# Transposing ternary FFN weights by DMA instead of on TensorE, with the layer-norm transposes in f32

## The chip, the cores and the metric

The kernel runs on the 8 cores of one Trainium2 chip. Each core computes two of the 16 sequences of the batch and exchanges nothing with the others; every core prepares the weights for itself. The metric is the device time in microseconds of the slowest core.

## The reference

A transformer block without an output projection, over x of shape (16, 4096, 1024):

```python
xn = _layernorm(x, axis=-1)
x = x + attn(xn, Wq, bq, Wk, bk, Wv, bv) + ffn(xn, W1, b1, W2, b2)
...
def _ternary(w):
    scale = jnp.maximum(jnp.mean(jnp.abs(w)), 1e-08)
    return jnp.clip(jnp.round(w / scale), -1.0, 1.0)      # value in the forward pass
h = gelu(x @ _ternary(W1).T + b1)        # W1: (4096, 1024)
out = h @ _ternary(W2).T + b2            # W2: (1024, 4096)
```

The attention is full width (one head of 1024), with the scores masked to zero above the diagonal before the softmax. The kernel computes the row sums of the softmax and scales each token's own V row with their ratio to themselves; that part is the same in both versions.

## The kernel before, in words

A core owns 8192 tokens, in 32 supertiles of 256 (`NSUP`), handled in 16 pairs. The code writes one list of operations for each engine with a small emitter: `E(...)` adds a compute operation, `DMA(...)` a transfer. Each names what it reads and writes, and the emitter works out the semaphore waits. The order in a list is the order of emission, and all instructions are issued at one line (L708 in the profile), so groups are told apart by tile names. A `DMA` also waits until the semaphore it is given has seen its previous transfer finish (L96 and L97). SP issues the loads of weights, x and cached keys; POOL (GpSimd) issues the stores and the second weight stream of the preparation.

The order of the program (L673 to L692): x of supertiles 0 and 1 and their layer-norm statistics, attention of pair 0, the preparation of the weights (`emit_prep`), and then for every pair u: FFN of supertile 2u-2, FFN of 2u-1, attention of pair u; at last the FFNs of the last pair.

`emit_prep` (L228) has three passes over tiles of 1 MB of f32 weights, 16 tiles each. Pass one loads W1 (SP) and sums the absolute values on ScalarE, which gives the threshold. Pass two loads W1 again, makes each tile ternary with two VectorE operations (`tern_tile`, L256), transposes it in 16 blocks of 128x128 on TensorE into PSUM, and ScalarE copies it into `w1t_sb`, where all of W1 transposed stays for the rest of the kernel. Beside it POOL loads W2 into one of two halves of `ktbuf` and ScalarE sums it. Pass three (L315) loads W2 again, makes it ternary, transposes it on TensorE, ScalarE copies it into `ktbuf`, and POOL stores it transposed to HBM, in `w2t` of shape (4096, 1024).

`emit_ffn` (L568) handles one supertile. For each of 32 slices f of the hidden layer: `emit_h(f)`, 8 matmuls of 256 columns with `w1t_sb` and a GELU on ScalarE into `hT`; `emit_o2(f)`, 4 matmuls of 512 columns of `hT` with `w2buf` into `ps_o2a` and `ps_o2b`. `w2buf` holds two chunks of W2 transposed, each good for two slices; chunk k+2 is loaded from `w2t` (`load_w2chunk`, L575) once `emit_o2(2k+1)` has freed its place:

```python
emit_o2(f - 2)
if (f - 2) % 2 == 1 and (f - 2) // 2 + 2 < 16:
    load_w2chunk((f - 2) // 2 + 2)
if f == 4:
    emit_v(1)
emit_h(f)
```

`emit_v` (L625) is the V projection of 128 tokens with the fused residual.

`emit_ln_finish` (L392) normalizes x into `xnbf` in bf16 and keeps a bf16 copy of x in `xbfres`. `emit_attn_pair` (L429) transposes `xnbf` on TensorE into PSUM, viewed as bf16, and VectorE copies it into `xnt`; then come Q, K and the scores. For the second half of a pair, `emit_ln_finish` stands inside `emit_attn_pair`.

Of the kernel before, what the change touches and what calls it, by code (L numbers as in the profile page):

```python
# [14 lines left out]
D = 1024  # L15
FF = 4096
# [85 lines left out]
def build_program(nc, B, SEQ):  # L102
# [15 lines left out]
    id_h = nc.dram_tensor("ident", [128, 128], BF16, kind="ExternalInput")  # L118
# [6 lines left out]
    w2t_h = nc.dram_tensor("w2t", [FF, D], BF16, kind="Internal")  # L125
# [19 lines left out]
    xnbf = sb("xnbf", [128, 2048], BF16)  # L145
# [15 lines left out]
    ident = sb("ident_sb", [128, 128], BF16)  # L161
# [12 lines left out]
    psqk_bf = ps_qk[:].bitcast(BF16)  # L174
    pss_bf = ps_s[:].bitcast(BF16)
# [52 lines left out]
    def emit_prep():  # L228
# [24 lines left out]
        t1v, t1k = w2buf[:, 0:2048], ["w2buf:0"]  # L253
# [14 lines left out]
        for tt in range(16):  # L268
# [6 lines left out]
            tbf = psqk_bf if tt % 2 == 0 else pss_bf  # L275
            tkeys = ["psqk:0", "psqk:1"] if tt % 2 == 0 else ["pss:0", "pss:1"]
            grp = []
            for u in range(2):
                for j in range(NJ):
                    k = u * NJ + j  # L280
                    grp.append(("transpose",
                                (tbf[:, k * 128:(k + 1) * 128],
                                 wtv[:, u * 1024 + j * 128:u * 1024 + (j + 1) * 128],
                                 ident[:]), {}))
            E("tensor", None, None, group=grp, reads=wtk + ["ident"], writes=tkeys)
            for u in range(2):
                E("scalar", "copy",
                  (w1t_sb[:].rearrange("p (j f) -> p j f", j=NJ)[:, :, (tt * 2 + u) * 128:(tt * 2 + u + 1) * 128],
                   tbf[:, u * 1024:(u + 1) * 1024].rearrange("p (j c) -> p j c", j=NJ)),
                  reads=tkeys, writes=["w1t"])  # L290
            ktf32 = ktbuf[:].bitcast(F32)
            j2, qq2p = divmod(tt, 2)
            buf2 = ktf32[:, (tt % 2) * 2048:(tt % 2 + 1) * 2048]
            bkey2 = [f"ktbuf:{tt % 2}"]
            DMA("gpsimd", s_gp[tt % 4], buf2,
# [4 lines left out]
              reads=bkey2, writes=["dump:0", "dump:1", f"acc:{tt}"])  # L300

# [13 lines left out]
        for qq2 in range(2):  # L315
            for j in range(NJ):
                tt = qq2 * 8 + j
                buf, bkey = pB(tt % 2), pkeys[tt % 2][0:2]
                DMA("sync", s_pl[tt % 4], buf,
                    w2_h.ap()[j * 128:(j + 1) * 128, qq2 * 2048:(qq2 + 1) * 2048],  # L320
                    writes=bkey)
                wtv, wtk = tern_tile(buf, bkey[0], 2, 3, tt % 2)
                tbf = psqk_bf if tt % 2 == 0 else pss_bf
                tkeys = ["psqk:0", "psqk:1"] if tt % 2 == 0 else ["pss:0", "pss:1"]
                grp = []
                for fs in range(16):
                    grp.append(("transpose",
                                (tbf[:, fs * 128:(fs + 1) * 128],
                                 wtv[:, fs * 128:(fs + 1) * 128],
                                 ident[:]), {}))  # L330
                E("tensor", None, None, group=grp, reads=wtk + ["ident"], writes=tkeys)
                stage = ktbuf[:, (j % 2) * 4096:(j % 2) * 4096 + 2048]
                skey = f"ktbuf:{j % 2}"
                E("scalar", "copy", (stage, tbf[:, 0:2048]),
                  reads=tkeys, writes=[skey])
                DMA("gpsimd", s_gp[tt % 4],
# [342 lines left out]
    if NSUP > 2:  # L679
        emit_x_loads(2)  # L680
    emit_prep()
    for u in range(1, NP):
# [5 lines left out]
        if 2 * u + 2 < NSUP:  # L688
            emit_x_loads(2 * u + 2)
# [68 lines left out]
```

How the kernel before makes its waits and increments, by code:

```python
        def go(eng):  # L702
            for waits, group, (s, amt) in lst:
                for ws, wv in waits:
                    eng.wait_ge(ws.h, wv)
                last = None
                for method, args, kwargs in group:
                    last = getattr(eng, method)(*args, **kwargs)
                if last is not None and s is not None:
                    last.then_inc(s.h, amt)
```

## Time and profile before

| | us |
|---|---|
| time, median of 2 runs | 3693.57 (3692.96 to 3694.18) |
| time of the profiled execution | 3707.41 |
| span of its slowest core (core 7) | 3705.9 |
| spans of its eight cores | 3645.7 to 3705.9 |
| TensorE busy in it | 3179.7 (86%) |
| ScalarE, VectorE busy in it | 1153.2, 559.8 |

The profile is of one execution and one core, the slowest; times in it count from the start of the span. PE is TensorE, PEld its weight loads, DVE VectorE, ACT ScalarE, SPq the queue of DMA issues on SP. The granted clock is a share of the full one.

### The profile page before, as it was taken

The page shows a single profiled execution, that of the slowest core. Times are in us where ns is not written, and L with a number is a line of the kernel's source. Part 1 is how long each engine was busy: PE and PEld are TensorE (multiplying, and loading weights), DVE is VectorE, ACT ScalarE, POOL GpSimd, SP SyncE. Part 2 cuts the span into 40 slices and gives each one's busy share as a digit, 9 for nine tenths or more (in the row PEclk, how much of TensorE's full clock was granted, in tenths as well). Part 3 has the DMA queues.
Part 4 walks back from the last instruction along what each step waited for, and adds up shares of the span by engine and source line. Part 5 has one row for each costly group of instructions (what it writes and reads, how often), then busy time and mean ns, then how long its engine had stood idle before and what let it go on. Part 6 is the DMA issues. An engine that isn't in the chain of part 4 may idle for free.

```text
span 3705.9 us, 57742 instructions; the slowest of 8 cores (3645.7 to 3705.9 us)
## 1 busy us (share of the span) xinstructions
PE 3179.7 (86%) x21512; PEld 2054.4 (55%) x21512; DVE 559.8 (15%) x1036; ACT 1153.2 (31%) x2414; POOL 97.9 (3%) x135
## 2 busy tenths in 40 slices
PE   3123899999998989999899989899898999989899
PEld 2122566665665565556555656566565565555655
DVE  1055211102011100201002020201110110101000
ACT  1453323232333232332323223233323233332332
POOL 0001000000000000000000000000000000000000
PEclk9555899999999999999999999999999999999999
DMA  6798533425252443424434252525243333534334
GB/s 126 215 293 252 170 126 117 145 92 160 78 158 85 148 120 112 156 74 156 121 105 160 86 166 75 171 75 165 75 152 121 120 120 108 162 95 137 114 110 141
DMA packets 298512, 496.66 MB, mean 134 GB/s; under 512 B 14596, under 2 KB 129284, under 8 KB 294150
## 3 DMA queue, kind: packets, MB, share of 16 engines
q1 hardware_dynamic: 276694, 411.19, 35.8%
q0 software_dynamic: 21552, 81.80, 7.3%
q8 instruction: 183, 3.00, 0.3%
q14 instruction: 83, 0.68, 0.1%
HBM read 440.50 MB, written 58.72 MB: 135 GB/s over the span
## 4 chain that ended last, share of the span: by engine, by line
PE 71%; DMA 19%; DVE 4%; issue 3%; ACT 2%; SPq 0%; DVEq 0%; ACTq 0%; POOL 0%; POOLq 0%
PE ps_qk L708 37%; PE ps_s L708 12%; PE ps_o2a L708 11%; PE ps_o2b L708 10%; DMA w2buf<-w2t 9%; DMA ktbuf<-kthbm 4%; ACT dump L708 2%; DMA xld<-w 2%; DMA outst<-w 2%; DMA xld<-x 1%; DVE w2buf L708 1%; DVE xnbf L708 1%; DVE xnt L708 1%; DVE outst L708 1%; DVE dump L708 1%
## 5 line engine op out<-in xcount | busy, mean ns | idle before, releaser
L708 PE MATMUL ps_qk<-xnt,w1t_sb 128*128 128x256 bf16 x8192 | 1060.8, 273 | 18.4 <-DVE msk L708 18.4
L708 PEld LDWEIGHTS ps_qk<-xnt,w1t_sb 128*128 128x128 bf16 x8192 | 800.9, 98 | 325.4 <-issue 24.0
L708 ACT ACTIVATE hT<-ps_qk,b1l 128x256 bf16<-128x256 f32 x1024 | 482.2, 474 | 1529.7 <-PE ps_qk L708 1529.3
L708 PE MATMUL ps_o2a<-w2buf,hT 128*128 128x512 bf16 x2048 | 610.0, 379 | 52.3 <-DMA w2buf<-w2t 50.7
L708 PE MATMUL ps_o2b<-w2buf,hT 128*128 128x512 bf16 x2048 | 609.8, 379 | 0.0
L708 PEld LDWEIGHTS ps_o2b<-w2buf,hT 128*128 128x128 bf16 x2048 | 200.1, 98 | 242.6 <-issue 1.1
L708 PE MATMUL ps_qk<-xnt,wq_sb 128*128 128x256 bf16 x2048 | 257.6, 294 | 18.5 <-DVE xnt L708 18.5
L708 PEld LDWEIGHTS ps_o2a<-w2buf,hT 128*128 128x128 bf16 x2048 | 189.0, 98 | 121.3 <-issue 99.7
L708 PE MATMUL ps_s<-ktbuf,qt 128*128 128x512 bf16 x896 | 214.8, 395 | 44.2 <-DMA ktbuf<-kthbm 44.0
L708 DVE TENSOR_SCALAR sts<-sts 128x1 f32<-128x1 f32 (+1 forms) x194 | 29.3, 152 | 1466.4 <-ACT dump L708 1457.6
L708 PEld LDWEIGHTS ps_qk<-xnt,wq_sb 128*128 128x128 bf16 x2048 | 214.7, 105 | 61.1 <-issue 22.3
L708 PE MATMUL ps_s<-wv_sb,xnt 128*128 128x512 bf16 x1024 | 243.2, 380 | 0.0
L708 PE MATMUL ps_qk<-xnt,wk_sb 128*128 128x256 bf16 x2048 | 226.2, 273 | 0.0
L708 PEld LDWEIGHTS ps_qk<-xnt,wk_sb 128*128 128x128 bf16 x2048 | 200.4, 98 | 23.2
L708 PE MATMUL ps_qk<-ktbuf,qt 128*128 128x512 bf16 x896 | 202.5, 379 | 0.0
L708 PEld LDWEIGHTS ps_s<-ktbuf,qt 128*128 128x128 bf16 x896 | 89.0, 101 | 161.6 <-issue 71.2
L708 ACT ACTIVATE qt<-ps_qk,bql 128x512 bf16<-128x512 f32 x128 | 88.0, 688 | 286.1 <-PE ps_qk L708 286.1
L708 PE MATMUL ps_qk<-ident_sb,xnbf 128*128 128x128 bf16 x512 | 50.3, 265 | 146.7 <-DVE xnbf L708 146.6
L708 DVE TENSOR_TENSOR msk<-ps_s,trilm_sb 128x128 bf16<-128x128 f32 x32 | 9.3, 292 | 1013.7 <-PE ps_s L708 1003.3
L708 PEld LDWEIGHTS ps_s<-wv_sb,xnt 128*128 128x128 bf16 x1024 | 89.6, 98 | 119.7 <-issue 29.0
L708 PEld LDWEIGHTS ps_qk<-ktbuf,qt 128*128 128x128 bf16 x896 | 87.6, 98 | 105.7
L708 ACT ACTIVATE ktcur<-ps_qk,bkl 128x512 bf16<-128x512 f32 x128 | 88.0, 687 | 135.6 <-PE ps_qk L708 135.6
(70 smaller groups left out, 1615.5 us busy)
## 6 DMA issues: line engine op xcount, KB each, us to landing
w2buf<-w2t SPq DMA_DIRECT2D x512, 512.0 KB, 3.7
ktbuf<-kthbm SPq DMA_DIRECT2D x112, 512.0 KB, 4.7
xld<-x SPq DMA_DIRECT2D x64, 512.0 KB, 5.5
out<-outst POOLq DMA_DIRECT2D x64, 512.0 KB, 3.7
outst<-w SPq DMA_DIRECT2D x24, 1024.0 KB, 7.5
xld<-w SPq DMA_DIRECT2D x24, 1024.0 KB, 7.4
kthbm<-ktcur POOLq DMA_DIRECT2D x32, 512.0 KB, 3.9
ktbuf<-w POOLq DMA_DIRECT2D x16, 1024.0 KB, 8.2
```

Source lines behind the costliest of these rows:

```text
L708: last = getattr(eng, method)(*args, **kwargs)
```

## The change

It does four things. The ternary W1 is no longer transposed on TensorE: POOL stores each ternary tile as it is to `w1tern`, and when all 16 are stored, SP issues eight DMA transposes of 4096x128 each into `w1t_sb`. The ternary W2 is stored as it is to `w2tern`, and each chunk that an FFN loads is now two DMA transposes of 1024x128, issued by SP on the one semaphore of that chunk's place. In pass two the W2 stream has one buffer (`xld`) and not two halves of `ktbuf`. The layer norm writes f32 in place over x in `xld`, after the copy to `xbfres`; the transposes of it are f32, go to `ps_qk` and `ps_s` in turn, and `ident` is f32. Because `xld` now holds the normalized x until it is transposed, the loads of x for the next pair stand behind the attention.

```diff
@@ emit_prep, pass two
-            E("tensor", None, None, group=grp, reads=wtk + ["ident"], writes=tkeys)
-            for u in range(2):
-                E("scalar", "copy",
-                  (w1t_sb[...], tbf[:, u * 1024:(u + 1) * 1024]...),
-                  reads=tkeys, writes=["w1t"])
+            DMA("gpsimd", s_gp[tt % 4],
+                w1tern_h.ap()[tt * 256:(tt + 1) * 256, :].rearrange("(two p) c -> p two c", p=128),
+                wtv.rearrange("p (two c) -> p two c", two=2),
+                reads=wtk, writes=[f"w1tern:{tt}"])
-            buf2 = ktf32[:, (tt % 2) * 2048:(tt % 2 + 1) * 2048]
-            bkey2 = [f"ktbuf:{tt % 2}"]
+            buf2 = xld[:, 0:2048]
+            bkey2 = ["xld00", "xld01"]
...
+        for j in range(NJ):
+            DMA("sync", s_tp[j % 2], w1t_sb[:, j * FF:(j + 1) * FF],
+                w1tern_h.ap()[:, j * 128:(j + 1) * 128],
+                reads=[f"w1tern:{t}" for t in range(16)], writes=["w1t"], transpose=True)
@@ emit_prep, pass three
-                E("tensor", None, None, group=grp, reads=wtk + ["ident"], writes=tkeys)
-                E("scalar", "copy", (stage, tbf[:, 0:2048]), reads=tkeys, writes=[skey])
-                DMA("gpsimd", s_gp[tt % 4], w2t_h.ap()[...], stage..., reads=[skey], writes=[f"w2t:{qq2}:{j}"])
+            DMA("gpsimd", s_gp[tt % 4],
+                w2tern_h.ap()[j2 * 128:(j2 + 1) * 128, qq2p * 2048:(qq2p + 1) * 2048],
+                wtv,
+                reads=wtk, writes=[f"w2tern:{qq2p}:{j2}"])
@@ emit_ln_finish
-            E("vector", "tensor_scalar",
-              (xnbf[:, i * 1024:(i + 1) * 1024], buf, mean, rstd, ALU.subtract, ALU.mult),
-              reads=[bkey, meank, rstdk], writes=[f"xnbf:{i}"])
             E("vector", "tensor_copy",
               (xbfres[:, p * 2048 + i * 1024:p * 2048 + (i + 1) * 1024], buf),
               reads=[bkey], writes=[f"xbfres:{p}:{i}"])
+            E("vector", "tensor_scalar",
+              (buf, buf, mean, rstd, ALU.subtract, ALU.mult),
+              reads=[bkey, meank, rstdk], writes=[bkey])
@@ emit_attn_pair
-                                (psqk_bf[:, i * 1024 + j * 128:i * 1024 + (j + 1) * 128],
-                                 xnbf[:, i * 1024 + j * 128:i * 1024 + (j + 1) * 128],
+                                (pst[:, j * 128:(j + 1) * 128],
+                                 xbuf[:, j * 128:(j + 1) * 128],
                                  ident[:]), {}))
@@ load_w2chunk
-            DMA("sync", s_w2[wb],
-                w2buf[:, wb * 2048:(wb + 1) * 2048].rearrange("p (ft c) -> p ft c", ft=2),
-                w2t_h.ap()[k * 256:(k + 1) * 256, :].rearrange("(ft p) c -> p ft c", p=128),
-                reads=[f"w2t:{k // 8}:{j}" for j in range(NJ)], writes=[f"w2buf:{wb}"])
+            for u in range(2):
+                ft = 2 * k + u
+                DMA("sync", s_w2[wb],
+                    w2buf[:, wb * 2048 + u * 1024:wb * 2048 + (u + 1) * 1024],
+                    w2tern_h.ap()[:, ft * 128:(ft + 1) * 128],
+                    reads=[f"w2tern:{ft // 16}:{j}" for j in range(NJ)],
+                    writes=[f"w2buf:{wb}"], transpose=True)
@@ order of the program
+        emit_attn_pair(u)
         if 2 * u + 2 < NSUP:
             emit_x_loads(2 * u + 2)
-        emit_attn_pair(u)
```

The queue of SP, with its waits, at the start of the first FFN before the change; `s_w20` and `s_w21` are the semaphores of the two places in `w2buf`, sP is TensorE's, sV VectorE's, `s_gp0` to `s_gp3` those of POOL's transfers:

```order
63 L708 DMA w2buf<-w2t 128x2x1024 [waits s_gp0,s_gp1,s_gp2,s_gp3,sV,sP]
64 L708 DMA w2buf<-w2t 128x2x1024 [waits sV]
65 L708 DMA w2buf<-w2t 128x2x1024 [waits s_w20,sP]
66 L708 DMA w2buf<-w2t 128x2x1024 [waits s_w21,sP]
67 L708 DMA w2buf<-w2t 128x2x1024 [waits s_w20,sP]
```

The same place in SP's queue after the change:

```order
71 L687 DMA_TRANSPOSE w2buf<-w2tern 128x1024 [waits s_gp0,s_gp2,sV]
72 L687 DMA_TRANSPOSE w2buf<-w2tern 128x1024 [waits s_w20]
73 L687 DMA_TRANSPOSE w2buf<-w2tern 128x1024 [waits sV]
74 L687 DMA_TRANSPOSE w2buf<-w2tern 128x1024 [waits s_w21]
75 L687 DMA_TRANSPOSE w2buf<-w2tern 128x1024 [waits s_w20,sP]
76 L687 DMA_TRANSPOSE w2buf<-w2tern 128x1024 [waits s_w20]
77 L687 DMA_TRANSPOSE w2buf<-w2tern 128x1024 [waits s_w21,sP]
```

Each load has become two, and the second of a chunk stands behind a wait for the first one's semaphore.

VectorE's queue in the first attention pair before the change, from the first half's layer norm to the last copy of a transpose:

```order
L708 TENSOR_SCALAR xnbf<-xld,sts 128x1024
L708 CAST xbfres<-xld 128x1024
L708 TENSOR_SCALAR xnbf<-xld,sts 128x1024
L708 CAST xbfres<-xld 128x1024
L708 COPY xnt<-ps_qk 128x8x128 x2
```

And VectorE's queue for the same half after the change:

```order
L687 CAST xbfres<-xld 128x1024
L687 TENSOR_SCALAR xld<-xld,sts 128x1024
L687 CAST xbfres<-xld 128x1024
L687 TENSOR_SCALAR xld<-xld,sts 128x1024
L687 CAST xnt<-ps_qk 128x8x128
L687 CAST xnt<-ps_s 128x8x128
```

The copy to `xbfres` now stands ahead of the operation that the transposes wait for, and the copies from PSUM read f32.

## Rows read from the trace of the kernel before

**Rows 1.** The page: busy tenths and granted clock in 40 slices.

```profile
PE 3179.7 (86%) x21512; PEld 2054.4 (55%) x21512; DVE 559.8 (15%) x1036; ACT 1153.2 (31%) x2414; POOL 97.9 (3%) x135
...
PEclk9555899999999999999999999999999999999999
```

**Rows 2.** Waits by engine, in us, times and longest: TensorE on `w2buf`.

```profile
PE ps_o2a L708 <- DMA w2buf<-w2t: 50.7, 66, 2.4
```

**Rows 3.** Timeline of TensorE, 701 to 709 us: start, duration, group, idle before.

```profile
701.81 0.59 PE L708 MATMUL ps_o2a<-w2buf,hT 128*128 128x512 bf16 x2
...
704.54 0.59 PE L708 MATMUL ps_o2a<-w2buf,hT 128*128 128x512 bf16 x2 [0.83 <-DMA w2buf<-w2t]
704.97 0.59 PE L708 MATMUL ps_o2b<-w2buf,hT 128*128 128x512 bf16 x2
705.40 1.04 PE L708 MATMUL ps_qk<-xnt,w1t_sb 128*128 128x256 bf16 x8
706.27 0.59 PE L708 MATMUL ps_o2a<-w2buf,hT 128*128 128x512 bf16 x2
```

**Rows 4.** DMA issues of the whole run: count, KB each, median us to landing.

```profile
w2buf<-w2t SPq DMA_DIRECT2D x512, 512.0 KB, 3.7
...
ktbuf<-w POOLq DMA_DIRECT2D x16, 1024.0 KB, 8.2
w2t<-ktbuf POOLq DMA_DIRECT2D x16, 512.0 KB, 6.6
```

**Rows 5.** The tile `w2buf`: its loads' shortest, median and longest time to landing.

```profile
DMA to landing us min/median/max: 3.3/3.7/9.0
```

**Rows 6.** Stretches holding two FFNs: busy us, granted clock, DMA share, GB/s.

```profile
390.00:455.00 65.00, 63.56 (x407) 38.55 (x405) 5.03 (x6) 15.93 (x34) 0.88 (x1) 1.00 0.46 138
455.00:520.00 65.00, 63.45 (x412) 39.39 (x411) 10.78 (x18) 18.94 (x41) 1.43 (x2) 1.00 0.49 152
```

**Rows 7.** Stretches holding passes two and three of the preparation, same columns.

```profile
182.00:296.00 114.00, 30.57 (x260) 26.64 (x260) 58.65 (x35) 62.40 (x64) 7.40 (x14) 0.50 0.89 285
296.00:387.00 91.00, 29.79 (x257) 26.24 (x258) 59.02 (x33) 27.99 (x15) 17.12 (x15) 0.50 0.83 249
```

**Rows 8.** Groups by form: busy us, mean ns of one, idle before.

```profile
L708 DVE SCALAR_TENSOR_TENSOR dump<-xld,sts,w2buf 128x2048 bf16<-128x2048 f32 x16 | 37.6, 2351 | 11.0 <-ACT dump L708 9.2 <-DVE w2buf L708 1.7
L708 ACT ACTIVATE dump<-ktbuf 128x2048 bf16<-128x2048 f32 x16 | 30.6, 1912 | 0.0
L708 PE MATMUL ps_s<-sts,onesf 1*128 1x2 f32 x4 | 1.1, 345 | 1.5 <-DVE sts L708 1.5
L708 DVE SCALAR_TENSOR_TENSOR outst<-ps_o2a,outst 128x1024 f32<-128x1024 f32 x32 | 39.2, 1224 | 97.2 <-PE ps_o2b L708 97.2
```

**Rows 9.** Timeline of one pair's transposes on TensorE and VectorE, 709 to 720 us.

```profile
709.80 1.06 PE L708 MATMUL ps_qk<-ident_sb,xnbf 128*128 128x128 bf16 x16
713.84 1.47 DVE L708 COPY xnt<-ps_qk 128x1024 bf16<-128x1024 bf16 x2
715.23 0.80 DVE L708 TENSOR_SCALAR xnbf<-xld,sts 128x1024 bf16<-128x1024 f32 x1
715.95 0.68 DVE L708 CAST xbfres<-xld 128x1024 bf16<-128x1024 f32 x1
716.28 1.01 PE L708 MATMUL ps_qk<-ident_sb,xnbf 128*128 128x128 bf16 x8 [5.42 <-DVE xnbf L708]
...
719.74 2.51 PE L708 MATMUL ps_qk<-xnt,wq_sb 128*128 128x256 bf16 x11 [1.12 <-DVE xnt L708]
```

**Rows 10.** Stretches around that pause: busy us by engine, granted clock, DMA share.

```profile
708.00:712.00 4.00, 2.86 (x26) 1.59 (x23) 1.18 (x7) 2.96 (x6) 0.00 (x0) 1.00 0.66 214
...
716.00:720.00 4.00, 2.29 (x18) 1.78 (x19) 3.25 (x6) 0.00 (x0) 0.00 (x0) 0.50 0.99 351
720.00:724.00 4.00, 4.00 (x21) 2.83 (x20) 0.00 (x0) 0.59 (x1) 0.00 (x0) 0.50 0.85 231
724.00:728.00 4.00, 4.00 (x35) 3.46 (x34) 0.00 (x0) 1.11 (x3) 0.00 (x0) 0.92 0.56 215
```

More of the change, by code:

```diff
@@ L124, in build_program @@
     w2tern_h = nc.dram_tensor("w2tern", [D, FF], BF16, kind="Internal")
-    w2t_h = nc.dram_tensor("w2t", [FF, D], BF16, kind="Internal")
     ctx = ExitStack()
@@ L274, in emit_prep @@
             wtv, wtk = tern_tile(buf, bkey[0], 0, 1, tt % 2)
-            tbf = psqk_bf if tt % 2 == 0 else pss_bf
-            tkeys = ["psqk:0", "psqk:1"] if tt % 2 == 0 else ["pss:0", "pss:1"]
-            grp = []
-            for u in range(2):
[L279 to L284, printed above, removed]
-            E("tensor", None, None, group=grp, reads=wtk + ["ident"], writes=tkeys)
-            for u in range(2):
-                E("scalar", "copy",
-                  (w1t_sb[:].rearrange("p (j f) -> p j f", j=NJ)[:, :, (tt * 2 + u) * 128:(tt * 2 + u + 1) * 128],
-                   tbf[:, u * 1024:(u + 1) * 1024].rearrange("p (j c) -> p j c", j=NJ)),
-                  reads=tkeys, writes=["w1t"])
-            ktf32 = ktbuf[:].bitcast(F32)
+            DMA("gpsimd", s_gp[tt % 4],
+                w1tern_h.ap()[tt * 256:(tt + 1) * 256, :].rearrange("(two p) c -> p two c", p=128),
+                wtv.rearrange("p (two c) -> p two c", two=2),
+                reads=wtk, writes=[f"w1tern:{tt}"])
             j2, qq2p = divmod(tt, 2)
-            buf2 = ktf32[:, (tt % 2) * 2048:(tt % 2 + 1) * 2048]
-            bkey2 = [f"ktbuf:{tt % 2}"]
-            DMA("gpsimd", s_gp[tt % 4], buf2,
+            buf2 = xld[:, 0:2048]
+            bkey2 = ["xld00", "xld01"]
+            DMA("gpsimd", s_gp[(tt + 2) % 4], buf2,
                 w2_h.ap()[j2 * 128:(j2 + 1) * 128, qq2p * 2048:(qq2p + 1) * 2048],
@@ L314, in emit_prep @@
         E("vector", "tensor_copy", (thrbc[:, 2:4], ps_s[:, 10:12]), reads=["pss:0"], writes=["thrbc"])
[L315 to L330, printed above, removed]
-                E("tensor", None, None, group=grp, reads=wtk + ["ident"], writes=tkeys)
[L332 to L336, printed above, removed]
-                    w2t_h.ap()[qq2 * 2048:(qq2 + 1) * 2048, j * 128:(j + 1) * 128].rearrange(
-                        "(fs p) c -> p fs c", p=128),
-                    stage.rearrange("p (fs c) -> p fs c", fs=16),
-                    reads=[skey], writes=[f"w2t:{qq2}:{j}"])
+        for tt in range(16):
+            j2, qq2p = divmod(tt, 2)
+            buf, bkey = pB(tt % 2), pkeys[tt % 2][0:2]
+            DMA("sync", s_pl[tt % 4], buf,
+                w2_h.ap()[j2 * 128:(j2 + 1) * 128, qq2p * 2048:(qq2p + 1) * 2048],
+                writes=bkey)
+            wtv, wtk = tern_tile(buf, bkey[0], 2, 3, tt % 2)
+            DMA("gpsimd", s_gp[tt % 4],
+                w2tern_h.ap()[j2 * 128:(j2 + 1) * 128, qq2p * 2048:(qq2p + 1) * 2048],
+                wtv,
+                reads=wtk, writes=[f"w2tern:{qq2p}:{j2}"])
     NSUP = B * NST
@@ L441, in emit_attn_pair @@
             for i in range(2):
+                pst = ps_qk if i == 0 else ps_s
+                tkeys = ["psqk:0", "psqk:1"] if i == 0 else ["pss:0", "pss:1"]
+                xbuf = xld[:, p * 2048 + i * 1024:p * 2048 + (i + 1) * 1024]
                 grp = []
@@ L678, in build_program @@
     emit_attn_pair(0)
+    emit_prep()
     if NSUP > 2:
         emit_x_loads(2)
-    emit_prep()
     for u in range(1, NP):
```

16 lines of the change are left out of this document (6 added, 10 removed).

## The prediction

> **What bounds the kernel now.** I read the slices first. TensorE is busy eight or nine tenths of every slice but the first four, and there its granted clock falls to half (1.2 instead of 2.4 GHz) [rows 1]. So the kernel has two parts: a preparation of weights in which transfers and VectorE set the pace, and some 3300 us in which TensorE sets it. The waits come second. TensorE waits for `w2buf` only 50.7 us in all, 66 times, 2.4 us at most [rows 2]. The loads of W2 are therefore hidden, but barely. The timeline shows how barely. One chunk of `w2buf` serves two slices, and a slice takes 0.87 us for `emit_o2` and 0.87 us for `emit_h`: 704.54 to 705.40 and 705.40 to 706.27 [rows 3]. A slice is 704.54 to 706.27, 1.73 us, and a chunk lasts 3.47 us. From the moment its place is free until the chunk is needed again TensorE has three `emit_h` and two `emit_o2` to do, 5 x 0.87 = 4.34 us, and the load lands in 3.7 us [rows 4]. The margin is 0.6 us, and where a load is late, TensorE stands, 0.83 us in one place [rows 3]. An FFN takes about 65 us [rows 6], 32 of them 2080 us. Anything that lengthens a chunk's load past 4.3 us is paid on the path, up to 512 times.
>
> **W2 by DMA transposes.** A chunk is now two transposes, and the second is not issued before the first has landed, because both use the semaphore of their place. Call T the time from issue to landing of one transpose of 256 KB. A place goes through T + T for the load and then `emit_o2`, `emit_h`, `emit_o2`, 2.6 us, until it is free. Two places alternate, so a chunk can't come more often than every P = (2T + 2.6)/2 = T + 1.3 us. SP waits with everything behind it while a first half is in flight, which sets P no shorter than T and adds nothing. P stays within 3.47 us only if T is 2.2 us, and a late chunk is avoided altogether only if T is 2.17 us, half of 4.34.
>
> The trace has no DMA transpose, so T must be bounded. From below: the plain load of 512 KB lands in 3.7 us [rows 4], and 256 KB at the same rate would be 1.85 us. From above: the longest landing of any load into `w2buf`, 9.0 us [rows 5], for a transfer that shares its engines badly. The nearest row is the store `w2t<-ktbuf`, 512 KB cut into pieces of 256 bytes: 6.6 us [rows 4]. The transpose reads pieces of 256 bytes as well (128 columns of bf16), half as many: between 3.3 us if the time goes by pieces and 6.6 us if it doesn't. I take the middle, T = 5.0 us.
>
> What TensorE does then matters too. With T = 5.0 and full clock P is 6.3 us and TensorE stands 2.8 us of it in one piece. In this trace a pause of 0.83 us costs no clock, while one of 5.42 us does: the granted clock is 0.50 from 716 to 724 us and back at 0.92 only in the next stretch, after 4 us and more of dense work [rows 9, 10]. In the preparation, where TensorE is busy 27% of the time in short pieces, it is 0.50 throughout [rows 7]. An FFN of 3.5 us of work and 2.8 us of pause lies between these rows, nearer to the preparation in its pattern. I take half clock. Then the work between landing and free place is 5.2 us and P = T + 2.6 = 7.6 us.
>
> An FFN pair has 32 chunks, of which the first two of the FFN that follows an attention are loaded under that attention. So a pair costs 30 x P + 6 us (the two `emit_h` and the V projection ahead of the first chunk). For 16 pairs: 16 x (30 x 7.6 + 6) = 3744 us, against 2080 us now. Term: +1664 us. With full clock it is 16 x (30 x 6.3 + 6) = 3120, +1040 us.
>
> At this place the Trainium skill speaks against itself. "Advanced Engine Details and Errata", section X-Bar Transpose (TRN2), has transposes as fast as ordinary transfers, at 350 to 400 GB/s; by it 256 KB are 0.75 us on the wire, and T would be that of a plain load (rival two). "VectorE: DVE Perf Modes", section The three transpose paths, gives 1309 ns for one 128x128 block by DMA; eight of them in a row would be 10.5 us, and the estimate of the whole would lie above rival three. No run here shows either yet.
>
> **The preparation.** Pass two takes 114 us and its transfers run at 285 GB/s [rows 7]. It loses the TensorE transposes and 32 ScalarE copies, which lie beside the transfers and give nothing back while these set the pace. It gains 8 MB of stores. The W2 stream has one buffer now, so load, sum and next load are a chain: for two tiles two loads of 8.2 us [rows 4], two sums of 1.9 + 0.2 us, a ternary operation of 2.35 us [rows 8] between them (the odd tile goes to `dump`, which the sum also writes, and POOL issues in order), and about 2 us of issues: 25 us, 200 us for the pass, +86 us. If loads land faster with fewer in flight, nothing is lost. I take +55 us, between 0 and 86.
>
> The eight transposes of W1 are 8 MB, 32 times 256 KB, two in flight: 32 x 5.0 / 2 = 80 us. SP does nothing else meanwhile and pass three's loads are queued behind it, so all of it is on the path; bounds 30 us (T = 1.85) and 144 us (T = 9.0). Pass three takes 91 us [rows 7], set by load and VectorE (59 of its 91 us busy); TensorE and ScalarE leave it and that gives nothing. Its first two loads are no longer under way when the threshold is known, and the first FFN must wait for a store and two transposes: +10 us, between 0 and 20. Together +145 us.
>
> **The layer norm.** Moving x's loads behind the attention costs nothing: they are needed at the end of the next FFN, 65 us later. On the path is the stretch from the end of an FFN to the Q projection, 709.80 to 719.74 us, 16 times (in the first pair TensorE has no FFN before it) [rows 9]. Three things grow. The copy to `xbfres` now precedes the normalization (+0.68 us). The copies out of PSUM read f32: 1.22 us, as the row that reads 1024 f32 from PSUM has it [rows 8], for 0.69 us. And the transposes are f32: eight in bf16 take 1.01 us [rows 9]; the two f32 matmuls of the preparation stand in the trace as four [rows 8], so a factor of two is the least likely to be missed; I bound the group by 1.01 and 4 us and take 3 us. Followed through: first half done at 715.8, second copy until 717.0, CAST and normalization until 718.5, two groups of 3 us until 724.5, copy until 725.7. That is +6 us for a pair, +96 us for 16 (bounds 0.7 and 10 us, 11 and 160 us).
>
> **Sum.** 3707.4 + 1664 + 145 + 96 = 5612 us for the profiled execution. The median of the runs is 13.8 us below the profiled one, so 5598; I say 5600 us.
>
> **The rivals.**
> One, T near the low end by pieces, 3.3 us, with full clock because the pauses are 1.1 us. P = 4.6, the FFNs take 16 x (30 x 4.6 + 6) = 2304, +224; preparation 55 + 53 + 10; layer norm 96. Total +438: 4130 us. For it: the DMA engines are busy only 0.46 of an FFN [rows 6]. Between it and the forecast lies T = 5.0 with full clock, 3694 + 1040 + 145 + 96 = 4975 us.
> Two, the other side: transposes land like plain transfers, T under 2.2 us, and stay hidden in the 4.34 us between a free place and its use. Then the FFNs keep their 2080 us, W1 costs 30, the layer norm 11: 3735 us, within 2% of now; if the 50.7 us of waits went as well, 3684. It decides at T = 2.17 us. Against it: no load of 512 KB landed in under 3.3 us [rows 5], and two latencies in a row have to fit.
> Three, a transpose is worked off slowly, T = 9.0 us or more. P = 11.6 at half clock, the FFNs take 16 x (30 x 11.6 + 6) = 5664, +3584; preparation 55 + 144 + 10; layer norm 96: 7580 us. For it: small pieces on both sides, 1024 rows read and columns of two bytes written, on eight cores at once.
>
> **How the numbers follow.** The forecast and its surroundings, 4700 to 6700 us (T from 4 to 7, either clock), 0.45. Rival one, 3900 to 4700, 0.22. Rival three, above 6700, 0.30. Rival two 0.03. The range goes from 4150 us (a little above rival one) to 7700 us (a little above rival three at 9.0 us), which leaves out about 2 in 10. A measurement of this kernel can tell some 2% from no change. Slower by more than that 0.96, within 0.03, faster 0.01.
>
> **What would show it.** In the changed kernel: `w2buf<-w2tern` with 1024 issues and its time to landing, which is T itself; TensorE's waits for `w2buf` in the thousands of us instead of 50.7; the granted clock in an FFN, 0.5 for my forecast and 1.0 for rival one; SPq waiting for `w2buf` transfers and not for TensorE. Chunk to chunk the timeline should show T + 1.3 or T + 2.6 us. The layer norm's stretch should be about 16 us long instead of 10, and a stretch of some 80 us with only DMA work should stand between passes two and three. The prediction is wrong if T is below 2.2 us, or if several transposes in flight slow each other so that P follows the rate and not T; then T itself grows in the trace.

## The result and the profile after

The changed kernel takes 4839.34 us (median of 11 runs, 4827.84 to 5025.98) against 3693.5 us (10 runs) for the kernel before on the same chips: a ratio of 1.3112 (95% interval 1.3084 to 1.314), 1146 us more. The profiled execution took 4831.11 us, with a span of 4829.6 us on its slowest core (core 3). In some runs the cores of one die (four of the eight) showed a much lower clock than the other four; comparisons leave these runs out, and where an experiment's profile was such a run I read a core of the other die.

The page of the changed kernel, its parts 1, 2 and 4:

```profile
PE 3383.1 (70%) x21000; PEld 2088.6 (43%) x21000; DVE 603.4 (12%) x1036; ACT 1092.0 (23%) x2366; POOL 100.2 (2%) x151
...
PE   3000377787777878777787877787777878778787
...
PEclk9555689899999999899899999999999989999999
...
DMA packets 1275924, 513.57 MB, mean 106 GB/s; under 512 B 1120900, under 2 KB 1235716, under 8 KB 1271558
...
DMA w2buf<-w2tern 36%; PE ps_qk L687 21%; PE ps_s L687 8%; PE ps_o2a L687 6%; PE ps_o2b L687 5%; DMA xld<-w 3%; DMA ktbuf<-kthbm 3%; SPq L687 3%; ACT dump L687 2%; DVE xnt L687 1%; DMA w1t_sb<-w1tern 1%; DMA outst<-w 1%; DVE w2buf L687 1%; DVE outst L687 0%; DMA w2tern<-w2buf 0%
```

TensorE's tenths fall from eight and nine to seven and eight [rows 1], and the busiest piece of the chain that ends last is now the transposed loads of W2, 36% of the span. The clock row matters as much: it doesn't stay at half speed in the FFNs, as I had forecast, but near nine tenths. The waits say who stands. "SPq" is SP's issuing of DMAs; its two rows are its waits ahead of an issue:

```profile
PE ps_o2a L687 <- DMA w2buf<-w2tern: 853.5, 366, 100.5
...
PE ps_qk L687 <- DVE xld L687: 150.4, 17, 65.2
...
SPq L684 <- DMA w2buf<-w2tern: 1392.6, 512, 8.3
SPq L684 <- PE ps_o2b L687: 710.3, 200, 49.7
```

TensorE waits 853.5 us for `w2buf`, 50.7 before [rows 2]. The longest, 100.5 us, isn't in an FFN: it is the first `emit_o2` standing until the preparation is over. About 753 us are left, 702 more than before [rows 2]. SP waits for `w2buf` transfers 512 times, exactly once per chunk: that is the second half held back until the first has landed, 2.7 us at a time.

The groups of the FFN's matmuls (busy us, mean ns of one, idle before):

```profile
L687 PE MATMUL ps_qk<-xnt,w1t_sb 128*128 128x256 bf16 x8192 | 1149.4, 288 | 71.5 <-DMA w1t_sb<-w1tern 53.0
L687 PE MATMUL ps_o2a<-w2buf,hT 128*128 128x512 bf16 x2048 | 667.6, 410 | 709.3 <-DMA w2buf<-w2tern 709.1
...
L687 PE MATMUL ps_o2b<-w2buf,hT 128*128 128x512 bf16 x2048 | 669.0, 411 | 0.0
```

The same instructions took 1060.8, 610.0 and 609.8 us before. So they cost 205 us more of busy time, which is the clock at half speed in part of the FFN. Waits (702) and clock (205) make 907 us. The timeline gives the growth itself: the 16 pairs of FFNs, each from its first `emit_h` to its last `emit_o2` (the first pair from its first `emit_o2`, so without that long wait), take 3096 us in all against 2157 before, 939 more; the stretches between them (the attention) take 28 us more, and the first `emit_o2` starts 157 us later. Together that is the 1124 us between the two spans.

How long a transpose takes stands in two views, part 6 of the page and the tile `w2buf` (duration in ns of the issue on SP, then us to landing):

```profile
w2buf<-w2tern SPq DMA_TRANSPOSE x1024, 3.6
...
w1t_sb<-w1tern SPq DMA_TRANSPOSE x8, 7.7
```

```profile
L687 SPq DMA_TRANSPOSE w2buf<-w2tern x1024: 1143/1147/2776, 542.5 to 4815.6; - x171
...
DMA to landing us min/median/max: 3.0/3.6/12.0
```

T, the time from issue to landing of one transpose, has a median of 3.6 us. The chain of waits at one place in the first FFN pair shows how two of them stack up (start, us, what):

```profile
604.34 4.83 DMA w2buf<-w2tern
609.24 4.21 DMA w2buf<-w2tern
613.45 0.14 issue
613.58 1.01 PE ps_o2a L687 x2
614.59 0.85 PE ps_o2b L687 x2
615.45 1.69 PE ps_qk L687 x8
617.13 0.43 PE ps_o2a L687 x2
617.56 0.45 PE ps_o2b L687 x2
618.04 0.04 issue
618.08 5.00 DMA w2buf<-w2tern
```

Two landings in a row, 9.0 us; then `emit_o2`, `emit_h`, `emit_o2`, 4.5 us; then the place is free and the next first half is issued. That is 13.74 us for two chunks, P = 6.87, where P is the time from chunk to chunk. It is one of the slow ones. Over chunks 4 to 15 of all 32 FFNs a chunk comes every 5.6 us: the two landings take 3.76 and 3.55 us in the mean, the work from `emit_o2` to the free place 3.0 us, and about 0.9 us lies between them (between the halves, from landing to `emit_o2`, from the free place to the next issue). 314 of these 384 chunks are late by more than 0.2 us. The first `emit_o2` and the `emit_h` after it run at half clock (1.01 us and 1.69 us), the second one at full clock again. The timeline of TensorE later in the run shows that this is not always so:

```profile
2791.99 1.01 PE L687 MATMUL ps_o2a<-w2buf,hT 128*128 128x512 bf16 x2 [3.68 <-DMA w2buf<-w2tern]
...
2795.03 0.59 PE L687 MATMUL ps_o2a<-w2buf,hT 128*128 128x512 bf16 x2
...
2804.17 0.59 PE L687 MATMUL ps_o2a<-w2buf,hT 128*128 128x512 bf16 x2 [3.76 <-DMA w2buf<-w2tern]
...
2806.83 1.06 PE L687 MATMUL ps_o2a<-w2buf,hT 128*128 128x512 bf16 x2
2807.68 0.92 PE L687 MATMUL ps_o2b<-w2buf,hT 128*128 128x512 bf16 x2
```

After these pauses of 3.7 us the clock is at half speed for some 3 us, at once or a little later, and full again. Behind a pause of 2.50 us a little earlier (2779.44 us) the same two matmuls take 0.59 us, so it stays full there. The stretches of the preparation (pass two, the W1 transposes, pass three):

```profile
182.00:377.00 195.00, 0.00 (x0) 0.00 (x0) 55.13 (x31) 30.03 (x30) 21.86 (x31) 0.50 0.58 196
380.00:440.00 60.00, 0.74 (x4) 0.61 (x4) 0.62 (x4) 2.00 (x2) 0.00 (x0) 0.50 0.84 151
440.00:542.00 102.00, 8.27 (x34) 3.80 (x34) 58.12 (x32) 2.13 (x3) 9.38 (x15) 0.53 0.84 255
```

Pass two takes 195 us (114 before), the transposes 60, pass three 102 (91 before) [rows 7]. In pass two the DMA engines are now busy 0.58 instead of 0.89: a chain has replaced a rate. The first `emit_o2` starts at 552.4 instead of 395.6 us, 157 us later. Last, the layer norm between FFN and attention:

```profile
763.70 1.04 PE L687 MATMUL ps_qk<-ident_sb,xld 128*128 128x128 f32 x8
...
766.25 1.22 DVE L687 CAST xnt<-ps_qk 128x1024 bf16<-128x1024 f32 x1
...
770.64 1.94 PE L687 MATMUL ps_qk<-ident_sb,xld 128*128 128x128 f32 x8 [5.03 <-DVE xld L687]
...
775.86 1.36 PE L687 MATMUL ps_qk<-xnt,wq_sb 128*128 128x256 bf16 x11 [1.65 <-DVE xnt L687]
```

From the first transpose to the Q projection it takes 12.2 us, 9.9 before [rows 9]. The f32 transposes take twice the time of the bf16 ones. At full clock eight of them take 1.04 us, where before the change sixteen took 1.06 us (709.80 us in [rows 9]); at half clock eight take 1.94 us, where before they took 1.01 us (716.28 us there, with a granted clock of 0.50 in [rows 10]). From start to start it is 109 against 56 ns at full clock, and 217 against 100 ns at half.

### The profile page after: what moved, and what is told of

The parts are those of the page before. It is cut to its first block, busy times and chain, and to the rows that moved or that the text cites. A ratio compares the mean times of both kernels' runs of the same rounds, so it can differ in the third digit from the quotient of the medians.

```text
span 4829.6 us, 57552 instructions; the slowest of 8 cores (4705.6 to 4829.6 us)
## 1 busy us (share of the span) xinstructions
PE 3383.1 (70%) x21000; PEld 2088.6 (43%) x21000; DVE 603.4 (12%) x1036; ACT 1092.0 (23%) x2366; POOL 100.2 (2%) x151
## 4 chain that ended last, share of the span: by engine, by line
DMA 47%; PE 41%; DVE 4%; SPq 3%; issue 3%; ACT 2%; DVEq 0%; ACTq 0%; POOL 0%; POOLq 0%
DMA w2buf<-w2tern 36%; PE ps_qk L687 21%; PE ps_s L687 8%; PE ps_o2a L687 6%; PE ps_o2b L687 5%; DMA xld<-w 3%; DMA ktbuf<-kthbm 3%; SPq L687 3%; ACT dump L687 2%; DVE xnt L687 1%; DMA w1t_sb<-w1tern 1%; DMA outst<-w 1%; DVE w2buf L687 1%; DVE outst L687 0%; DMA w2tern<-w2buf 0%
## 5 line engine op out<-in xcount | busy, mean ns | idle before, releaser
L687 PE MATMUL ps_qk<-xnt,w1t_sb 128*128 128x256 bf16 x8192 | 1149.4, 288 | 71.5 <-DMA w1t_sb<-w1tern 53.0
L687 PE MATMUL ps_o2a<-w2buf,hT 128*128 128x512 bf16 x2048 | 667.6, 410 | 709.3 <-DMA w2buf<-w2tern 709.1
L687 PEld LDWEIGHTS ps_qk<-xnt,w1t_sb 128*128 128x128 bf16 x8192 | 846.3, 104 | 451.5 <-issue 146.4
L687 PE MATMUL ps_o2b<-w2buf,hT 128*128 128x512 bf16 x2048 | 669.0, 411 | 0.0
L687 PEld LDWEIGHTS ps_o2b<-w2buf,hT 128*128 128x128 bf16 x2048 | 213.0, 104 | 284.4 <-issue 74.3
L687 PE MATMUL ps_qk<-xnt,wq_sb 128*128 128x256 bf16 x2048 | 241.9, 283 | 26.8 <-DVE xnt L687 26.8
L687 ACT ACTIVATE dump<-xld 128x1024 bf16<-128x1024 f32 (+1 forms) x88 | 112.5, 1281 | 204.1 <-DMA xld<-w 193.5
L687 PE MATMUL ps_qk<-ident_sb,xld 128*128 128x128 f32 x256 | 48.5, 353 | 150.4 <-DVE xld L687 150.4
```

Source lines behind the costliest of these rows:

```text
L687: last = getattr(eng, method)(*args, **kwargs)
```

## The experiments

Twelve kernels ran. Times are of the whole kernel, and each ratio is to the kernel before, run beside it (3684 to 3691 us). A difference between two kernels is the difference of their ratios times 3690 us.

### The two halves of a chunk

**e1_own_sem.** The changed kernel, with a semaphore and a key of its own for each half of a place. `emit_o2(f)` waits for its own half and frees it by itself.

```diff
-    s_w2 = [em.sem("s_w20"), em.sem("s_w21")]
+    s_w2 = [em.sem(f"s_w2{i}") for i in range(4)]
...
-                DMA("sync", s_w2[wb],
+                DMA("sync", s_w2[2 * wb + u],
...
-                    writes=[f"w2buf:{wb}"], transpose=True)
+                    writes=[f"w2buf:{wb}:{u}"], transpose=True)
...
-            reads = [f"hT:{bank}", f"w2buf:{wb}"]
+            reads = [f"hT:{bank}", f"w2buf:{wb}:{f % 2}"]
```

> The changed kernel, with a semaphore and a tile key for each half of a chunk, so that SP issues the second transpose of a chunk right behind the first and does not wait for its landing. Theory chain (the loss in the FFNs is two landings in a row, 4.85 and 4.12 us in the chain of waits of the changed kernel): a chunk then lands 1.15 us (the issue) + 4.5 us = 5.7 us after its place is free, not 9.0, and chunks can come every (5.7 + 2.6) / 2 = 4.2 us. Most of the 930 us goes: 3900 to 4100 us in all. Theory rate (the crossbar or the DMA engines work transposes off at a fixed rate, so more in flight only take longer each): the landing grows to 6 us and more, a chunk still comes every 5.9 us, and the time stays at 4700 to 4850 us.

Measured: 1.0441 (1.0416 to 1.0466), about 3850 us: 985 us of the 1146 are gone (0.2671 x 3690). Waits of TensorE and landings of the same transposes, on core 0:

```profile
PE ps_o2a L687 <- DMA w2buf<-w2tern: 104.8, 9, 102.0
```

```profile
DMA to landing us min/median/max: 2.9/4.0/12.1
```

Of the 104.8 us 102.0 are the wait for the preparation, so 2.8 us are left in 32 FFNs (7.3 on core 1). The same bytes in the same pieces go through the same queue, each transpose lands later than before (4.0 us, on cores 1 and 3 4.4, for 3.6), and almost nothing waits. In a stretch of the first FFN pair TensorE is busy 98.81 of 100 us at full clock, with the DMA engines busy 0.85 of the time (0.48 in 600 to 700 us of the changed kernel):

```profile
560.00:660.00 100.00, 98.81 (x646) 63.29 (x656) 10.96 (x18) 30.25 (x63) 1.07 (x2) 1.00 0.85 158
```

So it was a chain of latencies and not a rate: if transposes had limited each other, four in flight would have gained little. The chain theory held, and the gain was larger than it had expected.

**e8_own_whole.** e1's semaphores and keys, but `emit_o2` waits for both halves and frees both, as in the changed kernel. This tells which half of e1 does it.

```diff
-            reads = [f"hT:{bank}", f"w2buf:{wb}:{f % 2}"]
+            reads = [f"hT:{bank}", f"w2buf:{wb}:0", f"w2buf:{wb}:1"]
```

> As e1_own_sem (a semaphore for each half, no wait between the two issues of a chunk), but o2 waits for both halves of its chunk and so also frees both together. It separates not waiting at issue from the earlier free place. Theory: a chunk lands about 1.15 + 4.5 = 5.7 us after it is free, 4.34 us are covered, chunks come every 4.15 us: +100 to +250 us against e1_own_sem, 3950 to 4100 us. Rival: only the wait between the issues mattered: 3850 to 3880 us, as e1_own_sem.

Measured: 1.1496 (1.1477 to 1.1515), 4234 us, 389 us more than e1 and well above what I expected. A late chunk in its chain:

```profile
608.51 1.15 SPq L687
609.75 5.41 DMA w2buf<-w2tern
615.29 0.59 PE ps_o2a L687 x2
```

Both halves go out together, but the second is issued 1.15 us after the first, since SP is busy that long with a transpose, and lands 5.4 us later here. From the first issue that is 6.7 us, more than the 4.34 us of cover. So not being held at the issue is worth 596 us (1.3112 to 1.1496), and halves that come free one by one another 389 us (1.1496 to 1.0441). What held the issue was the shared semaphore and the shared key together; they were not tried apart.

**e3_split_plain.** The kernel before, its chunk loaded as two plain transfers of 256 KB on the one semaphore. It has the new order of waits without any transpose.

```diff
-            DMA("sync", s_w2[wb],
-                w2buf[:, wb * 2048:(wb + 1) * 2048].rearrange("p (ft c) -> p ft c", ft=2), ...
+            for u in range(2):
+                DMA("sync", s_w2[wb],
+                    w2buf[:, wb * 2048 + u * 1024:wb * 2048 + (u + 1) * 1024],
+                    w2t_h.ap()[k * 256 + u * 128:k * 256 + (u + 1) * 128, :],
+                    reads=[...], writes=[f"w2buf:{wb}"])
```

> The kernel before, with each plain load of a chunk (512 KB) split into two plain loads of 256 KB on the one semaphore of its place, no transposes by DMA. Theory chain: what costs is two landings in a row, whatever the transfer is. A plain 256 KB should land in 2.3 to 3 us, two in a row take 4.6 to 6 us against the 4.34 us that are covered, chunks come every (2T + 2.6) / 2 = 3.6 to 4.3 us instead of 3.47: +70 to +350 us. Theory transpose (only the transposing is slow): no change, 3690 to 3720 us.

Measured: 1.0902 (1.0874 to 1.093), 4019 us, +333 us. Its part 6 and a wait:

```profile
w2buf<-w2t SPq DMA_DIRECT2D x1024, 256.0 KB, 2.7
```

```profile
PE ps_o2a L709 <- DMA w2buf<-w2t: 323.9, 361, 3.5
```

Half the bytes land in 2.7 us, not in half of 3.7 [rows 4]: by this difference 1.0 us goes with 256 KB and 1.7 us of a landing doesn't (an estimate). With T = 2.7 and full clock the formula of the prediction gives P = 4.0 for 3.47, 16 x 30 x 0.53 = +254 us. The mean landing in the trace is 2.9 us, and with it the formula gives +350 us, against 333 measured. So a third of the loss on W2 (333 of 962 us, by e4 below) needs no transpose at all.

**e5_before_halves.** The kernel before, with e3's split and e1's semaphores and keys.

> The kernel before (plain loads, W2 transposed on TensorE), with each chunk loaded in two halves that have a semaphore and a tile key of their own, so that a half is loaded again as soon as its own o2 has read it. Theory: what made own semaphores so good in the changed kernel (TensorE waited for w2buf in the FFNs for a few us only, less than before the change) is that a half place is free one o2 and one h earlier; here that removes the 50.7 us of waits for w2buf: -45 us, about 3648 us, the fastest of all. Rival: 1024 transfers instead of 512 take more of the DMA engines, and the waits only move to the cached keys: 3690 us, no change.

Measured: 0.9857 (0.9832 to 0.9882), 3634 us. TensorE's waits for `w2buf` have left the list. The two plain halves that cost 333 us on one semaphore gain 53 us on two.

**e9_before_both.** e5, and the same for the two 512 KB loads of a chunk of `ktbuf` in the attention.

```diff
-                DMA("sync", s_kt[cb],
+                DMA("sync", s_kt[2 * cb + gg],
...
-                    writes=[f"ktbuf:{cb}"])
+                    writes=[f"ktbuf:{cb}:{gg}"])
...
-                  reads=["qt", f"ktbuf:{cb}"], writes=[bkey_ps])
+                  reads=["qt", f"ktbuf:{cb}:0", f"ktbuf:{cb}:1"], writes=[bkey_ps])
```

> e5_before_halves (the kernel before with own semaphores for the halves of a W2 chunk), and the same for the cached keys: the two transfers of a ktbuf chunk get a semaphore each, so that SP issues the second without waiting for the first to land. Theory: SP waits 290 us for ktbuf transfers in the kernel before and TensorE 44 to 49 us for ktbuf; with both in flight at once most of the latter goes, -20 to -45 us against e5_before_halves, 3590 to 3610 us. Rival: the wait is the first chunk's after the stores of keys and for the freed buffer, not the second transfer's: no change, 3630 us.

Measured: 0.9728 (0.9714 to 0.9743), 3587 us, the fastest kernel of this study and some 1250 us below the changed one. Its waits:

```profile
PE ps_s L709 <- DMA ktbuf<-kthbm: 12.6, 10, 4.1
...
SPq L706 <- DMA ktbuf<-kthbm: 1.5, 7, 0.3
```

In e5 these two were 49.3 and 294.8 us. One load of `ktbuf` now lands in 6.9 us instead of 5.0, but two are in flight at a time, and TensorE waits less for the pair.

### The clock

**e6_spare_mm.** The changed kernel with eight matmuls ahead of every even `emit_o2` from slice 8 on, into a PSUM bank that is free there. Their results are not used; they are work beside the computation.

```diff
+            if f % 2 == 0 and f >= 8:
+                E("tensor", None, None,
+                  group=[("matmul", (ps_s[:, 0:512], xntv[:, 0:128], wv_sb[:, 0:512]),
+                          {"start": True, "stop": True})] * 8,
+                  reads=[xntk, "wv"], writes=["pss:0"])
```

> The changed kernel, with eight spare matmuls of 512 columns (1.7 us at full clock, into ps_s, which nothing reads then) ahead of each o2 of an even f from 8 on; their results are not used. They fill part of the pauses, so they price the clock. Theory clock: the 205 us by which the FFN matmuls are busier than before the change come from the half clock after pauses of 5 us; with shorter pauses the granted clock stays up (mean above 0.95 instead of 0.89) and the time falls by 50 to 200 us in spite of the added work. Theory no clock (the chunk rate is set by the two landings alone and a slow burst hides in the next one's landing): no gain, 4830 to 4900 us. If the spare work is itself in the way: above 4900 us.

Measured: 1.2897 (1.2871 to 1.2923), some 80 us faster than the changed kernel. The granted clock rises from 0.892 to 0.905 (over the cores) to 0.924 to 0.930, and the three groups above take 1089.0, 626.7 and 625.9 us: 144 of the 205 us are back. In this profile the FFN pairs take 3035 us against 3096. So the pauses do cost clock, and 80 us is what filling them gives net of the fillers' own time. The clock stayed below the 0.95 that I expected. Every chunk from slice 8 on has its filler, 12 of the 16 of an FFN, so the first four are as before; and the preparation, some 430 us at half clock, by itself keeps the mean of the changed kernel at 0.955 (an estimate from its trace).

### The rest: layer norm and preparation

**e2_ln_only.** The kernel before with the changed layer norm and its f32 transposes; the weights keep their path and have a bf16 identity of their own.

> The kernel before, with only the layer norm part of the change: f32 in place, copy to xbfres first, f32 transposes to ps_qk and ps_s in turn, loads of x behind the attention. Theory: the stretch from the last o2 to the Q projection is 12.2 us in the changed kernel and 9.9 us in the one before; 16 x 2.2 = +35 us, 3729 us. Rival, as the prediction had it, that the f32 transposes and the moved loads cost 6 us a pair: +96 us, 3790 us.

Measured: 1.0127 (1.0103 to 1.0151), 3733 us, +47 us. My 2.2 us were read in the changed kernel. In e2's own trace the stretch is 13.5 us in the mean against 9.8 before (718.84 to 732.56 us is one), +3.7 us, 56 us in 15 of them; TensorE's waits for `w2buf` fall by 15 us (35.3 for 50.7). The prediction's 6 us a pair was too much.

**e4_w2_plain.** The changed kernel with W2 transposed on TensorE and loaded plain, as before. What stays changed is the W1 path, pass two's single buffer and the layer norm.

> The changed kernel, with the W2 path of before (transposed on TensorE in pass three, stored, loaded plain in one transfer for each chunk); W1 by DMA transposes, one W2 buffer in pass two and the f32 layer norm stay. It splits the loss in two. Theory: the FFNs hold 930 us of it, preparation and layer norm the rest: 157 + 35 = +190 us, about 3885 us. Rival, that the preparation costs more because the DMA transposes of W1 and the stores delay what follows: over 3950 us.

Measured: 1.0506 (1.0481 to 1.0532), 3873 us, +187 us as expected. The W2 path is worth the difference to the changed kernel, some 962 us (0.2606 x 3690).

**e7_own_two_buf.** e1, with the W2 stream of pass two in the two halves of `ktbuf` as before.

> Own semaphores for the halves as in e1_own_sem, and in pass two the W2 stream goes to the two halves of ktbuf in turn, as before the change. Theory chain in pass two (load, sum, ternary, load: 26.5 us for two tiles): with two buffers pass two goes back from 195 us towards 120 to 130 us, because the transfers set the pace again and there are 8 MB more of them; 3854 - 65 = about 3790 us. Rival (the odd tile in dump waits for the store of w1tern, which lands in 7.6 to 10.4 us, and that is what makes pass two long): under 20 us gained, 3835 to 3855 us.

It has no ratio, and only one time to compare, 3829.09 us, 20 us below e1's two (3848.22 and 3850.28). Pass two on core 5:

```profile
195.34 2.35 DVE L687 SCALAR_TENSOR_TENSOR dump<-xld,sts,w2buf 128x2048 bf16<-128x2048 f32 x1 [11.30 <-ACT dump L687]
...
198.26 0.97 POOL L687 DMA_DIRECT2D w1tern<-dump  x1 [13.49 <-DVE dump L687]
...
212.73 1.91 ACT L687 ACTIVATE dump<-ktbuf 128x2048 bf16<-128x2048 f32 x1 [17.49 <-DMA ktbuf<-w]
...
236.29 1.91 ACT L687 ACTIVATE dump<-ktbuf 128x2048 bf16<-128x2048 f32 x1 [16.62 <-DMA ktbuf<-w]
```

Two tiles still take 23.6 us here (212.73 to 236.29), where the changed kernel has 25.9 at this place (211.75 to 237.68). The odd ternary tile is written to `dump` and stored from there; the sum of the next W2 tile writes `dump` too, so it can't start before that store has landed, and the next load stands behind it. From its first to its last ternary operation pass two takes 175 us, 196 in the changed kernel. My theory fell: the second buffer alone gives some 20 us of the 65 that I expected.

**e10_odd_in_qt.** e7, and the odd ternary tile in `qt`, which nothing uses in the preparation.

```diff
-                wtv, wtk = dump[:, 0:2048], ["dump:0", "dump:1"]
+                wtv, wtk = qt[:, 0:2048], ["qt"]
```

> e7_own_two_buf, and in passes two and three the odd ternary tiles go to qt (idle then) instead of dump. In e7 pass two still took 24 us for two tiles, because ScalarE's sum, whose output goes to dump, waited for the store of the odd tile out of dump. Theory: this store was the other half of pass two's chain; now the transfers set the pace again and pass two takes 125 to 145 us instead of some 190: -45 to -65 us, about 3770 us. Rival: three streams of transfers slow each other as much as the chain did: under 15 us gained, 3815 to 3830 us.

Measured: 1.024 (1.0221 to 1.0259), 3776 us, 74 us less than e1. Pass two takes 123 us by the same count, its DMA engines are busy 0.98 of the time, and the W1 transposes start at 303.65 us instead of 380.30:

```profile
182.00:300.00 118.00, 0.00 (x0) 0.00 (x0) 51.94 (x29) 28.03 (x28) 18.00 (x28) 0.50 0.98 322
```

**e11_w1_four** and **e12_w1_spread.** e10, first with a key for each of the eight W1 transposes and four semaphores, then also with each of them behind every second load of pass three.

```diff
-            DMA("sync", s_tp[j % 2], w1t_sb[:, j * FF:(j + 1) * FF],
+            DMA("sync", s_tp[j % 4], w1t_sb[:, j * FF:(j + 1) * FF],
...
-                ... writes=["w1t"], transpose=True)
+                ... writes=[f"w1t:{j}"], transpose=True)
```

> e10_odd_in_qt with a tile key for each of the eight DMA transposes of W1 and four semaphores, so that up to four are in flight; in the changed kernel each waits for the one before, because all write one key, and eight of 7.7 us in a row take 60 us. Theory row of landings: part of a landing is latency, so four in flight take 35 to 45 us in all, and the time falls by 15 to 25 us against e10 (3775 us), to 3755 us. Theory rate: transposes run at about 1 MB in 7 us (150 GB/s) whatever is in flight; the stretch stays at 50 to 60 us and the time within 5 us of e10, and each landing grows to over 20 us.

> The same, but the eight transposes of W1 are issued one after every second load of pass three instead of ahead of pass three. Theory: they lie beside VectorE's work in pass three, which leaves the DMA engines some room (busy share 0.84): of the 55 to 60 us 30 to 50 are hidden, 3725 to 3745 us. Rival: pass three is as long as its transfers, so 8 MB more lengthen it by what the transposes took: 3765 to 3780 us.

Measured: 1.0207 (1.019 to 1.0224), 3764 us, and 1.0202 (1.0166 to 1.0239), 3749 to 3776 us. Against e10 e11 gains some 12 us, at the edge of the two intervals; e12 can't be told from e11, and its middle lies between its two expectations (3725 to 3745 and 3765 to 3780 us). For e11 the latency theory is the nearer one: the stretch is at the top of its 35 to 45 us, and one landing takes 8.2 us, not over 20. SP's timeline in e11, and in e12:

```profile
304.90 44.62 SPq L687 DMA_TRANSPOSE w1t_sb<-w1tern  x8
```

```profile
323.26 16.89 SPq L688 DMA_TRANSPOSE w1t_sb<-w1tern  x1
```

With no wait between them the eight transposes still take 44.62 us to issue, 5.6 us each (54.57 us in e10). In e11 SP issues one behind the other without a pause, so there its issuing is the limit and not the landing. Whether an issue is long by itself or is held back by the transfers still in flight, no run tells. In e12, beside the loads of pass three, seven of the eight issues take 12.6 to 16.9 us each, and these loads are queued behind it, so spreading hides little.

## Why the prediction was right or wrong

**Direction and mechanism: right.** The forecast was slower, 5600 us; it is 4839, inside 4150 to 7700. The loads of W2 are late by the chain that the prediction wrote down (two landings in a row, then half of the work between landing and free place), and e1 shows that this chain holds them and no rate does. Rival two fell: T is 3.6 and not below 2.17 us. Rival three, slow working off, fell as well. Some of the signs that the prediction named for its forecast didn't show: the granted clock in the FFNs is near 0.9 and not 0.5, and the stretch of DMA work in the preparation is 60 us and not 80. Nor did that of the layer norm, 12 us and not 16.

**W2, forecast +1664 us, measured +939: too large by 725.** The prediction has 30P + 6 for a pair with P = 7.6, 234 us; the trace has 194 us and P = 5.6. Two terms were mis-sized. T was set at 5.0, the middle of 3.3 to 6.6 from the store `w2t<-ktbuf`; over the steady chunks its mean is 3.65, near the lower end of that range. That is 480 x 1.35, some 650 us too much. And TensorE was taken at half clock throughout, 5.2 us for the work between landing and free place, which takes 3.0: half of the difference, 1.1 us for each of 480 chunks, some 530 us too much. Two terms were left out, and they lie the other way. The 0.9 us between transfer and work are 0.45 us in P, some 215 us. And outside of its 30 chunks a pair takes 26 us and not 6, some 320 us: the interval between two chunks in which an FFN's second V projection stands is 7.8 us in both kernels, and the second FFN's first `emit_o2` stands 10 us behind the first FFN's last. Of these 320 us 77 are in the kernel before as well, whose pairs take 2157 us and not 2080. With all four the sum is off by some 720 us, which is the miss.

So a part of the nearness is luck. What T and the clock turned out to be is close to rival one (3.3 us and full clock), whose 4130 us is 700 too low: with T = 3.65 and 3.0 us of work the formula gives P = 5.15 and 16 x (30 x 5.15 + 6) = 2568 us, +488, half of what was measured. The two terms taken too large covered the two that were missing.

The row that I read for the clock, half speed from 716 to 724 after a pause of 5.42 us [rows 10], was right as it stands: the clock is back within a few us. It was wrong to liken the FFN to the preparation, where TensorE is busy a quarter of the time. Here it was busy three quarters.

The Trainium skill's two rules, that the prediction set against each other, can now be judged. "Advanced Engine Details and Errata", section X-Bar Transpose (TRN2), would have transposes as fast as plain transfers: 256 KB land in 3.6 us transposed and 2.7 us plain (e3), so not as fast, but nearer to it than the 5.0 us of my forecast. "VectorE: DVE Perf Modes", section The three transpose paths, has 1309 ns for one block: eight in a row would be 10.5 us (an estimate from it), and they land in 3.6, so the figure can't be multiplied by the number of blocks in one transfer.

**Preparation, forecast +145, measured +157: right in sum by luck, since two parts were wrong in opposite directions.** Pass two grew by 81 us, not 55. The chain of 25 us for two tiles was worked out rightly (195 us for eight of them, 24.4 each), with +86 as its end of the range, and I then took 55 because loads might land faster with fewer in flight; they didn't. I also had only a part of the cause: with the one buffer cured (e7) the store out of `dump` still holds two tiles for 17 to 24 us, and the pass is short only when both are gone (e10). The W1 transposes took 60 us, forecast 80 with two in flight. They are not two in flight: all eight write the key `w1t`, so each waits for the one before. They are in series at 7.4 us for 1 MB, where I had 20 us for each, two at a time: two errors against each other. Pass three, +10 forecast, +11 measured.

**Layer norm, forecast +96, measured +47 (e2).** The step that failed is the size of the f32 transposes, taken at 3 us for a group of eight. The row of 1.01 us for eight in bf16 is one at half clock [rows 9, 10], and in f32 a group at half clock takes 1.94: the factor is two, as the f32 matmuls of [rows 8] suggested, and I had taken three. Two groups of 1.06 us less are 2.1 of the 2.3 us between 6 and the 3.7 of e2. The copies from PSUM were right (1.22 us for 0.69), and so was moving x's loads at no cost, as far as a wait for them would have shown.

**The account of the 1146 us**, by differences of kernels: 596 the issue held at one semaphore (after to e8), 389 places that come free only whole (e8 to e1), 74 pass two (e1 to e10), 12 W1 in series (e10 to e11), and 76 that no version here took away (e11 to before). These 76 are a balance of larger parts. In e11's profile the first `emit_o2` starts at 459.6 us and not at 395.6, 64 later, and the stretches of attention are 42 us longer, which is the layer norm. The FFN pairs are 47 us shorter than before, 2110 us for 2157, because halves on their own semaphores also cure the waits that the kernel before had. So the preparation with W1 by DMA transposes still costs some 64 us. 45 us of them are the issuing on SP and 17 a longer pass two (121 us for 104, from the first to the last ternary operation); no kernel here tried either share by itself. With the same preparation as before, e3, e5 and e9 start at 381 to 389 us, so it may be 75. In the FFNs little is left of the transposes of W2 once the chain is gone: with plain halves (e5) the pairs take 2090 us.

## What to carry to other kernels

Before one transfer is split in two, look at what the second waits for. On the same semaphore as the first and in one buffer, a load that was hidden becomes two latencies in a row; with a semaphore and a key for each half the same split is free, and here it even beat the kernel it came from. A stream that is bound by latency leaves the DMA engines room while an engine waits for it (busy 0.48 in the changed FFNs, 0.58 in its pass two), and one experiment with more in flight tells it from a rate. And when a transfer reads or writes a buffer that it didn't touch before, list everything else that uses that buffer: in pass two two chains of nearly equal length lay beside each other, and curing one gave some 20 us, both together 74.

## What the runs showed that I had not expected

- The issue of a DMA transpose occupies SP: 1.15 us for 256 KB and 5.6 us for 1 MB (e11), up to 16.9 us beside other loads (e12), against 0.32 us for a plain load of 256 KB (e3). In no run were the eight transposes of 1 MB issued in less than 44.6 us.
- A transpose of 256 KB to landing takes 3.0 us at least and 3.6 in the median, 4.0 to 4.4 with up to four in flight (e1); one of 1 MB takes 7.7. Four times the data is twice the time.
- f32 transposes of 128x128 take twice what bf16 ones take at the same clock: 109 for 56 ns each at full clock, 217 for 100 ns at half. Rows of 1.04 us in f32 and 1.01 us in bf16 look alike only because the second is at half clock.
- After the two pauses of 3.7 us shown the clock was at half speed for some 3 us of work, and after one of 2.50 us it was not, so a kernel in which most chunks come late still had 0.89 to 0.91 of it over its span.
- The halves of a split load, each on its own semaphore, beat the single load of the kernel before: 0.9857 with W2, 0.9728 with `ktbuf` as well.
